# The qkv stage of a windowed-attention and ConvNeXt kernel: k cast in another element order, v widened on GpSimd, a part of q on ScalarE, stores issued by SyncE

## What is computed

```python
xw = x.reshape(B, C, r1, WS, r2, WS).transpose(0, 2, 4, 3, 5, 1).reshape(B * r1 * r2, n, C)
qkv = fq(xw) @ fq(Wqkv, axis=0).T + bqkv
q, k, v = jnp.split(qkv, 3, axis=2)
q = fq(q * SCALE); k = fq(k); v = fq(v)
...
attn = fq(fq(jnp.einsum('bhmc,bhnc->bhmn', q, k)) + bias[None])
out = jnp.einsum('bhmn,bhnc->bhmc', softmax(attn), v)
...
```

## Time and profile before

| | |
|---|---|
| median of the runs | 5791.29 us |
| the profiled execution's own time | 5786.68 us |
| its span, first to last instruction | 5785.0 us |
| mean granted TensorE clock | 0.824 of full speed |
| busy over the span | PE 75%, DVE 76%, ACT 54%, PEld 46%, POOL 26% |
| the qkv stage | from 442.1 us to about 917.6 us of the span |
| its bands | first v rounding at 465.87 us, last at 896.18 us |

### The profile page before, as it was taken

How to read it: one execution, slowest core, us unless ns; L and a number is a source line. 1 busy time by engine, 2 the same in 40 slices (tenths; PEclk the granted TensorE clock), 3 DMA queues, 4 the chain that set the end, 5 groups by cost and what they waited for, 6 DMA issues and landing times. The chain is left out here.

```text
span 5785.0 us, 117928 instructions
## 1 busy us (share of the span) xinstructions
PE 4339.0 (75%) x40394; PEld 2654.2 (46%) x40394; DVE 4400.3 (76%) x8162; ACT 3108.9 (54%) x5458; POOL 1506.0 (26%) x1649
## 2 busy tenths in 40 slices
PE   0887995555557777778764666999489898898988
PEld 0334553222236666666653453444244444444444
DVE  6998996999998888888885552000688888888885
ACT  0755661000038787778764564444466666666664
POOL 1103331000025565556553221000121212122120
PEclk9995555555569899999997778999789899998999
DMA  7754664333333333333325777887221221212221
GB/s 296 215 158 144 195 195 96 59 66 67 59 59 82 77 82 79 82 80 82 74 62 189 277 275 249 289 288 268 77 75 60 67 88 59 94 62 79 74 70 60
DMA packets 226274, 724.70 MB, mean 125 GB/s; under 512 B 34954, under 2 KB 132746, under 8 KB 205194
## 3 DMA queue, kind: packets, MB, share of 16 engines
q1 hardware_dynamic: 182346, 524.67, 31.5%
q0 software_dynamic: 43584, 195.21, 9.9%
HBM read 428.25 MB, written 291.50 MB: 124 GB/s over the span
## 5 line engine op out<-in xcount | busy, mean ns | idle before, releaser
L866 ACT ACTIVATE attn_int<-p_psum,scalars 128x588 int8<-128x588 f32 x512 | 384.3, 751 | 1047.3 <-PE p_psum L534 1021.9
L789 POOL TENSOR_TENSOR exp_lo<-exp,exp_hi 128x294 f16<-128x294 f32 x1024 | 775.6, 781 | 561.1 <-ACT exp_hi L860 558.8
L1574 ACT ACTIVATE gelu<-h_psum,b_rows,w_unscale 128x448 f32<-128x448 f32 x672 | 485.8, 723 | 510.1 <-PE h_psum L1490 348.4
L1525 PE MATMUL out_psum<-gelu_hi,w_parts 128*128 128x448 f16 x2016 | 622.5, 364 | 8.3 <-DVE w_parts L1711 4.4
L534 PE MATMUL range_psum<-q_diag,k_diag 128*128 128x196 bf16 x1536 | 364.9, 373 | 330.7 <-DVE p_min L652 328.5
L885 DVE SCALAR_TENSOR_TENSOR logit_int<-attn_int,scalars,bias_products 128x588 f16<-128x588 int8 x512 | 509.6, 996 | 124.8 <-ACT attn_int L866 97.8
L1617 DVE BATCH_NORM_STATS2 ln_stats<-z_img 128x6 f32<-128x192 f32 x448 | 125.5, 337 | 547.6 <-DMA z_img<-zd 547.5
L831 PE MATMUL o_psum<-a_v,exp_hi 128*128 128x34 f16 x6144 | 383.7, 179 | 207.1 <-DVE a_o L909 192.1
L1490 PE MATMUL h_psum<-ln_parts_T,w_hi 128*128 128x448 f16 x2016 | 501.4, 358 | 20.0 <-DVE w_in L1680 16.3
L1287 PE MATMUL conv_psum<-c_in,toeplitz 128*128 128x448 f16 (+1 forms) x2304 | 470.1, 366 | 60.6 <-DMA dwb<-in_L_conv_dw_b_dram 59.2
L1525 PE MATMUL out_psum<-gelu_lo,w_parts 128*128 128x448 f16 x1344 | 485.2, 361 | 0.0
(11 more groups left out here) (309 smaller groups left out, 9757.7 us busy)
## 6 DMA issues: line engine op xcount, KB each, us to landing
k_diag<-kd SPq DMA_DIRECT2D x128, 384.0 KB, 5.2
toeplitz<-gd SPq DMA_DIRECT2D x48, 1024.0 KB, 16.9
yd<-y_out POOLq DMA_DIRECT2D x16, 2880.0 KB, 25.9
c_in<-yd SPq DMA_DIRECT2D x24, 1920.0 KB, 9.2
zd<-c_out POOLq DMA_DIRECT2D x24, 1792.0 KB, 13.8
z_img<-zd SPq DMA_DIRECT2D x16, 2688.0 KB, 9.4
x_chunk<-in_x_dram SPq DMA_DIRECT2D x12, 3136.0 KB, 10.1
x_img<-in_x_dram SPq DMA_DIRECT2D x16, 2352.0 KB, 15.9
```

The lines of the kernel that those rows point to most:

```text
L789: last = nc.gpsimd.tensor_tensor(el[r][:, :, 2 * a, 0:N], src[:, :, a], eh[r][:, :, 2 * a, 0:N], ALU.subtract)
L866: nc.scalar.activation(a1[l % 2][:].rearrange("p (g n) -> p g n", g=G), pp[:, 0:G, 0:HG * N], ACT.Copy, scale=col(s, CP)).then_inc(a1d, 1)
L1525: last = nc.tensor.matmul(po[:, t, 0:TCH], w, hx[:, f, cols], start=f == 0 and x == 0, stop=f == NF - 1 and x == len(steps) - 1)
L1574: nc.scalar.activation(h[y % 3][:], ph[:, y % 3, 0:TCH], ACT.Gelu, scale=k1[:], bias=b1[:, f:f + 1]).then_inc(hd, 1)
```

## The change

- VectorE casts only the 128-row part of q, and the two parts of k. The k casts now walk the four windows first: four elements that follow each other in `k_out` are written in turn, and their int8 sources lie 49 bytes apart. One semaphore step per band (`qcv`) instead of four.
- ScalarE rounds j = 1 first, then 0 and 2 (TensorE makes them in that order), no longer widens v, and casts the 64-row part of q. It signals `qcs`.
- GpSimd widens v in two copies per band, behind a wait for `vev` and a one-element addition on a new tile `v_tick`.
- SyncE issues the six stores of a unit, right behind the load of the same buffer's next unit.

```diff
+        tick = sb("v_tick", [1, 1 + 2 * UB], F32)
...
@@ SyncE, in unit(i, first), behind the load
+                    if not first:
+                        store(i - 1, k)
+
+            def store(i, k):
+                sp.wait_ge(qcv, UB * (2 * i + k + 1))
+                sp.wait_ge(qcs, UB * (2 * i + k + 1))
+                sp.wait_ge(vcv, UB * (2 * i + k + 1))
...
+                sp.dma_start(qd[0:P], sq[k][:, 0]).then_inc(st[k], 16)
+                sp.dma_start(qd[P:C], sq[k][0:64, 1]).then_inc(st[k], 16)
+                sp.dma_start(kd[0:64], kk[64:P, 0]).then_inc(st[k], 16)
+                sp.dma_start(kd[64:C], kk[:, 1]).then_inc(st[k], 16)
+                for pl in range(2):
+                    sp.dma_start(vd[:, :, pl * 8:pl * 8 + 8, :], sv[k][pl * N:(pl + 1) * N]).then_inc(st[k], 16)
             peeled(sp, IMG, unit)
+            store(IMG - 1, 0)
+            store(IMG - 1, 1)
...
@@ GpSimd, in unit(i, first); the same six dma_start lines are gone from here
+                    if not first:
+                        pool.wait_ge(st[k], 16 * ND * i)
+                    for b in range(UB):
+                        pool.wait_ge(vev, 8 * i + 4 * k + b + 1)
+                        nc.gpsimd.tensor_tensor(tick[:, UB * k + b + 1:UB * k + b + 2], tick[:, 0:1], tick[:, 0:1], ALU.add)
+                        dst = sv[k][:].rearrange("p o j (h e) -> p o j h e", e=H1)[:, :, 2 * b:2 * b + 2, :, 0:HD]
+                        for o in range(2):
+                            last = nc.gpsimd.tensor_copy(dst[:, o], v8[b % 2][:, 2 * o:2 * o + 2, :].rearrange("p a (h e) -> p a h e", e=HD))
+                        last.then_inc(vcv, 1)
...
@@ TensorE and ScalarE
-                        for j in range(3):
-                            n = 3 * b + j
+                        for j in (1, 0, 2):
+                            n = 3 * b + (1, 0, 2).index(j)
...
@@ ScalarE
-                            act.wait_ge(qcv, 4 * (8 * i + 4 * k + b - 1))
+                            act.wait_ge(qcv, 8 * i + 4 * k + b - 1)
+                            act.wait_ge(qcs, 8 * i + 4 * k + b - 1)
...
-                        act.wait_ge(vev, 8 * i + 4 * k + b + 1)
-                        if not first:
+                        act.wait_ge(qev, 24 * i + 12 * k + 3 * b + 1)
+                        if not first and b == 0:
                             act.wait_ge(st[k], 16 * ND * i)
-                        dst = sv[k][:].rearrange("p o j (h e) -> p o j h e", e=H1)[:, :, 2 * b:2 * b + 2, :, 0:HD]
-                        for o in range(2):
-                            last = nc.scalar.copy(dst[:, o], v8[b % 2][:, 2 * o:2 * o + 2, :].rearrange("p a (h e) -> p a h e", e=HD))
-                        last.then_inc(vcv, 1)
+                        nc.scalar.copy(sq[k][0:64, 1, :, 4 * b * N:4 * (b + 1) * N],
+                                       i8[b % 2][0:64, 1, :].rearrange("p (o n) -> p o n", o=2)).then_inc(qcs, 1)
...
@@ VectorE
-                        for j, r0, r1 in ((0, 0, P), (1, 0, 64)):
-                            v.tensor_copy(sq[k][r0:r1, j, :, 4 * b * N:4 * (b + 1) * N],
-                                          q4[r0:r1, j, :].rearrange("p (o n) -> p o n", o=2)).then_inc(qcv, 1)
+                        v.tensor_copy(sq[k][:, 0, :, 4 * b * N:4 * (b + 1) * N], q4[:, 0, :].rearrange("p (o n) -> p o n", o=2))
                         for j, r0, r1 in ((1, 64, P), (2, 0, P)):
-                            v.tensor_copy(sk[k][r0:r1, j - 1, :, 0:N, 4 * b:4 * b + 4].rearrange("p o n a -> p o a n"),
-                                          q4[r0:r1, j, :].rearrange("p (o a n) -> p o a n", o=2, a=PAIRS)).then_inc(qcv, 1)
+                            last = v.tensor_copy(sk[k][r0:r1, j - 1, :, 0:N, 4 * b:4 * b + 4],
+                                                 q4[r0:r1, j, :].rearrange("p (o a n) -> p o n a", o=2, a=PAIRS))
+                        last.then_inc(qcv, 1)
```

More of the change, by code:

```diff
@@ L388, in phase_qkv @@
         ones, vr, ch = s.sem("xu_ones"), s.sem("v_row_psum"), s.sem("p1b_chain")
-        qmm, qev, qcv = s.sem("qk_product"), s.sem("qk_rounded"), s.sem("qk_placed")
+        qmm, qev, qcv, qcs = s.sem("qk_product"), s.sem("qk_rounded"), s.sem("qk_placed"), s.sem("q_rest_placed")
         vmm, vev, vcv = s.sem("v_product"), s.sem("v_rounded"), s.sem("v_placed")
@@ L401, in unit @@
                     sp.dma_start(xi[k][0:CK], src).then_inc(ld[k], 16)
+                    if not first:
[4 more added lines that the diff above has]
+                sp.wait_ge(vcv, UB * (2 * i + k + 1))
+                u = bass.ds(2 * i + k, 1)
+                qd = s.qd[u].rearrange("u f o n -> (u f) o n")
+                kd = s.kd[u].rearrange("u f o n -> (u f) o n")
+                vd = s.vd[u].rearrange("u o n j f -> n (u o) j f")
+                kk = sk[k][:].rearrange("p c o n j -> p c o (n j)")
+                sp.dma_start(qd[0:P], sq[k][:, 0]).then_inc(st[k], 16)
[4 more added lines that the diff above has]
+                    sp.dma_start(vd[:, :, pl * 8:pl * 8 + 8, :], sv[k][pl * N:(pl + 1) * N]).then_inc(st[k], 16)
             peeled(sp, IMG, unit)
+            store(IMG - 1, 0)
+            store(IMG - 1, 1)
+            for k in range(2):
+                sp.wait_ge(st[k], 16 * ND * IMG)
         @blk.gpsimd
@@ L406, in _ @@
             link = chain(pool, ones)
+            link(nc.gpsimd.memset(tick[:], 0.0))
             for k in range(2):
@@ L413, in unit @@
                 for k in range(2):
[L414 to L426, removed]
+                    if not first:
[7 more added lines that the diff above has]
+                        last.then_inc(vcv, 1)
             peeled(pool, IMG, unit)
-            for k in range(2):
-                pool.wait_ge(st[k], 16 * ND * IMG)
         @blk.tensor
         def _(pe):
-            pe.wait_ge(ones, 6)
+            pe.wait_ge(ones, 7)
             pe.wait_ge(ch, 2)
@@ L492, in _ @@
             link(v.tensor_copy(vrow[:, P:C], pq[:, 1, 0:64]))
-            dve.wait_ge(ones, 6)
+            dve.wait_ge(ones, 7)
             def unit(i, first):
```

## The result

The changed kernel takes 5728.11 us in the median of 3 runs (5720.04 to 5731.0), against 5791.29. The ratio is 0.9894, with a 95% interval from 0.9872 to 0.9917: 63 us less. The prediction was 5704 in a range of 5650 to 5797. The profiled execution's span is 5726.1 us, 58.9 under that of before.

A forecast was written before the change was run, and what follows sets the result against it. VectorE was taken to bound the qkv stage at 3.39 us a band; 1.09 + 1.20 + 0.45 = 2.74 saves 0.65, times 128 = 83 us. 5786.7 - 83 = 5704 us, range 5650 to 5797.

The forecast's parts named there:

- VectorE sets the pace; 3.39 us a band: In the qkv stage VectorE, with no idle time, bounds each band at 3.39 us, 434 us for 128 bands.
- 1.09 + 2D for the rest of the band: VectorE's v rounding 1.06, q cast 0.40 and two k casts, less 0.37 of overlap, in us a band.
- D = 0.60: Duration of one new-order k cast on VectorE: 0.60 us, between 0.35 (q cast) and 1.01 (old k cast).
- P = 0.50: Duration of one v copy on GpSimd: 0.50 us, between 0.42 and 0.99.
- 0.45 us of collisions: GpSimd's addition and first v copy delay VectorE's casts by 0.45 us a band; the second copy lies beside the next rounding.
- Stores costed at nothing: Moving the six stores of a unit to SyncE changes the time by nothing; the stage's end stays.
- Transfers fit, at 9.2 us of 11.0: Buffer reuse needs six SyncE issues, 3.5 us, and 5.7 to land: 9.2 of a unit's 11.0 us.
- faster still: Rival: copies hide beside the v rounding, D is 0.50, transfers bound a band at 2.2 us; 152 us saved, 5635; chance 0.13.
- TensorE's clock near 1.0: TensorE's granted clock in the stage rises to near 1.0 instead of 0.52, as it no longer waits.
- the rival in which TensorE becomes the bound: TensorE's clock stays at 1.2 GHz, a band is 3.21 us; 23 us saved, 5764; chance 0.06.
- slower: Rival: k-cast read hops cost what write hops did, D stays 1.01, band 3.56 us; 22 us more, 5809; chance 0.16.
- no change: Rival: addition and both copies block VectorE's casts at full length, 1.18 us; band 3.47, 10 us more, 5797; chance 0.09.

The follow-up runs named there:

- e11: Changed kernel with a third v copy of the same size on GpSimd, ahead of the two, into a spare tile; unit 13.52 us, run once, no ratio.
- e6: Kernel before with its six stores issued by SyncE and q and k casts counted once a band; ratio 0.9976 to the kernel before.
- e2: Kernel before with the new element order of the k casts and nothing else; ratio 0.9844 to the kernel before.
- e7: Kernel before with the new k order and stores on SyncE, v still on ScalarE, all q casts on VectorE; 5717.58 us, ratio 0.9848 to before.
- e3: Changed kernel without the two v copies on GpSimd, the one-element addition kept; ratio 0.9824 to the kernel before.
- e1: Changed kernel with the k casts back in their old element order; ratio 1.0117 to the kernel before.
- e4: Changed kernel with GpSimd's v copies also waiting until VectorE has placed that band's k; ratio 0.9937 to the kernel before.
- e10: e4 with VectorE's v rounding also waiting for GpSimd's one-element addition for the band before; ratio 0.9898 to the kernel before.
- e13b: e2 with the v stores of a unit issued ahead of those of q and k; ratio 0.9898 to the kernel before.
- e8: e2, stores on GpSimd, with each v store split into 48 rows and 1 row; ratio 0.9868 to the kernel before.

## Why the prediction held, point by point

The direction, the range and roughly the size held: 83 us forecast, 63 measured by the medians. That it came so near is in part luck. The band's saving was forecast at 0.65 us and is 0.46, the net of three terms that erred: two made it too large (0.08 and 0.32) and one too small (0.21). With the collisions alone at their measured size, the sum would have given 42 us. Over 128 bands that makes 59 us; the stage's end gives 6 more, and the later stages took 5.5 us back in the profiled pair. Neither was in the sum.

- **VectorE sets the pace; 3.39 us a band.** Held; it is the pace after as well, at 2.93.
- **1.09 + 2D for the rest of the band.** The constant is 2.93 - 0.99 - 0.77 = 1.17. The overlap of the rounding with the cast before it fell from 0.37 to 0.09, and the rounding itself, which was to stay at 1.17, got shorter by 0.22.
- **D = 0.60.** 0.49 to 0.50 for every cast in the new order that has no copies beside it. The new order costs 0.14 over the q cast's 0.35, not 0.25; that all of it is the hop between reads was taken for granted, and no run separates it from the step to the next row after each four writes. The writes of the old order lie 32 bytes apart, not 8. The estimate from the Trainium skill, "Vector Engine (DVE) Microarchitecture Reference", section 5.2, was 0.49 with its figure for one source that hops 4 KiB, 1.73 ns, and the trace agrees with it and not with the 0.64 from 2.5. Over both casts the sum was 0.21 too high.
- **P = 0.50.** 0.498.
- **0.45 us of collisions.** This is the step that was most in error: 0.77. It came from 0.63 of GpSimd's time for the addition and one copy, on the reading that the engines take turns. e11 shows that the copies run through: the first k cast waits for both, and ends 0.34 us after the second (706.08 against 705.74), where alone it lasts 0.49. The addition lies beside the q cast and costs it nothing (0.353). The second copy does not come out behind the casts, as the prediction had it. The sum was 0.32 too low here, 41 us over 128 bands.
- 2.74 + 0.08 - 0.21 + 0.32 = 2.93.
- **Stores costed at nothing.** Along the bands that nearly holds: e6's unit is 13.41 against 13.55, 4.4 us in all. But the end of the stage is over 6 us shorter, and with it the move alone is worth 10.8; with the new order (e2 and e7) the bands take that back.
- **Transfers fit, at 9.2 us of 11.0.** In the changed kernel VectorE does not wait for landed stores, and ScalarE does for 14.1 us in 310. The 2.2 us a band, taken from the transfers' busy share, was not the bound of the rival "faster still": in e3, where VectorE's own pace is 2.16 a band, a unit stops at 10.66, 2.67 a band.
- **TensorE's clock near 1.0.** It alternates, 0.83 on the mean. VectorE never waited for TensorE, so the rival in which TensorE becomes the bound did not come about.
- **Rival "slower", the hop changes sides.** Wrong: e2 shows 0.50 us. But e1 shows how near it was: with D at 1.01 the change loses 1.2%.
- **Rival "no change", full length.** Nearer in kind than the main case and wrong in size: both copies are in the first cast's way, for 0.77 us and not 1.18, and the shorter casts more than pay for it.

## What to carry to other kernels

A small reordering of an access pattern can be the whole gain, and work that is moved to another engine beside it can take part of the gain back: split a change into its parts before keeping all of it. Work given to GpSimd was not free for VectorE's SBUF-to-SBUF casts here, though GpSimd was busy for only 119.5 of 310 us; ask beside which instruction it will lie. Where buffers are reused only after the stores have landed, the transfers can hold a stage up long before their busy share is 1.

## What the runs showed of the hardware that was not expected

- A burst of GpSimd copies holds a VectorE cast off until its last one: 0.494, 1.272 and 1.721 us with none, two and three copies of 0.50.
- A v rounding, which reads PSUM and one SBUF operand, held a one-element addition of GpSimd with two SBUF inputs (1.04 us instead of 0.18, 0.918 on the mean in e4, the last part of it beside the q cast), but not the copies with one input (0.498 in e10), and was itself lengthened by neither (0.950 and 0.958). The Trainium skill, "SBUF — State Buffer", section "Who interferes with whom", has a VectorE instruction with at most one SBUF input, outside the modes that use both ports, not contend with GpSimd; for the copies the trace agrees, for the addition it does not.
- The same cast of 392 bytes to bf16 takes 0.35 us in order on both sides, 0.49 with reads 49 bytes apart and writes in runs of four, and 1.01 with reads in order and writes 32 bytes apart.
- In the kernels with all stores on SyncE the next stage begins 6.9 to 7.7 us after the end of their last issue. With the stores on GpSimd's queue it is 12.9 (before), 13.2 (e2) and 15.5 (e13b), but 6.3 in e8, which only cuts the v stores in two: it is not the queue alone, and the cause is open. The end of e8:

```profile
823.52 2.38 POOL L427 DMA_DIRECT2D vd<-v_out  x4
832.16 0.38 SPq L567 DMA_DIRECT2D rel_rows<-in_L_conv_rel_idx_dram  x1
```
